# Layer normalisation and one rotary sum of the second layer's projection stage, moved to VectorE

## The chip, the cores and the metric

One core of a Trainium2 chip runs the whole program. The metric is the device time of one execution in microseconds (us), smaller is better. The engines are TensorE (PE, its weight loads PEld), VectorE (DVE), ScalarE (ACT), GpSimd (POOL) and SyncE (SP, which here only issues DMAs). They run apart from one another, each in its own program order, and meet at semaphores.

## The reference

Two layers over x, 4 sequences of 2048 tokens, 256 channels:

```
xn = layernorm(x); x = x + rwkv_attention(xn) * silu(relu_ffn(xn))            # layer 0
xn = layernorm(x)                                                              # layer 1
c_q = xn @ W_DQ;  q = [c_q @ W_UQ, rope(c_q @ W_QR)]
c_kv = xn @ W_DKV; k = [c_kv @ W_UK, rope(xn @ W_KR)];  v = c_kv @ W_UV
s = causal_softmax(q k^T / sqrt(24)) v @ W_O                                   # 16 heads
xr, xk = mu * xn + (1 - mu) * xn_previous_token                                # two mixes
g = silu(sigmoid(xr @ W_r) * (relu(xk @ W_k)^2 @ W_v));  x = x + s * g
```

with layernorm(x) = (x - mean) / sqrt(var + 1e-5). A product xhat = x * rstd + (-mean * rstd) and xhat = (x - mean) * rstd are two ways to write the same normalisation.

## The kernel before, in words

Four stages follow each other, parted by barriers: layer 0 (about 0 to 689 us), the projections of layer 1 (689 to 1062), attention, and the output. The change lies in the second, `layer1_projections`. It works through 16 chunks of 512 tokens (4 tiles of 128 tokens by 256 channels), numbered n = 0 to 15. Each engine's order is written out by hand in its own `body(b, c, left)`, and `left` is the number of chunks still to come (capped at 4), so the last chunks drop the steps that prepare later ones.

What one body of each engine does, for chunk n:

- DVE: low halves of the latents (L1343, it reads PSUM), rotary products of the keys (L1349), low half of the query content (L1352), rotary products of the queries into q_cos and q_sin (L1356), low half of the key content (L1359), low half of the rotary queries (L1362: q_cos minus its half-precision copy), then for chunk n+2 the statistics (L1260), for chunk n+1 the two mixes (L1276: x_k twice, x_r twice) with the aggregation of chunk n+2 (L1267) between them, the low half of x_k (L1283), and the gate's product (L1373).
- POOL: rotary sum of the keys (L1126), square (L1129), rotary sum of the queries q_cos += q_sin (L1131), for chunk n+1 the token difference (L1101) and the low half of xn (L1106), low half of the rotary keys (L1136), for chunk n+2 `rstd_of`: var + eps (L1090), shift = -mean (L1091), rstd by pow (L1093), shift * rstd (L1095); then the low half of x_r of chunk n+1 (L1110) and the gate of chunk n (L1145).
- ACT: evictions and half-precision copies; `normalise` of chunk n+2 (L1175: four ACTIVATEs of 128x256, scale rstd, bias shift) stands after the latents (L1217) and ahead of the gate's sigmoid (L1248), the relu (L1224) and the query eviction (L1227).
- PE: latents, rotary keys, x_k product (12 matmuls), query products (8), `transposes` of the next chunk's xhat (L1393), x_r products in two halves around the key content product (4 matmuls), values, and the last product.
- SP: per chunk 4 stores of query content (L1040), 2 of rotary keys (L1043), 4 of key content (L1048), 2 of rotary queries (L1051), 1 of values (L1053), 1 of the gate (L1056), in this order, each kind behind a wait on the producer; a load of x (L1062) ahead of them while chunks are left. After chunk 12 it also issues the 20 loads of attention's first operands (`load_group`, L1487 and L1491).

A "low half" is the rest that a half-precision copy leaves: f32 value minus f16 copy. Layer 0 has its own `normalise`, on DVE (L455: four TENSOR_SCALARs of 128x256, subtract the mean, multiply by rstd).

Of the kernel before, what the change touches and what calls it, by code (L numbers as in the profile page):

```python
# [850 lines left out]
def layer1_projections(nc, a, d, ident, rows_out, early, scales, first):  # L851
# [6 lines left out]
    with ExitStack() as ctx:  # L858
# [44 lines left out]
        shift = sb("b_shift", [P, TPC])  # L903
        zeros = sb("b_zeros", [P, TPC])
# [73 lines left out]
        qr_sum = sem("b_qr_sum")  # L978
# [43 lines left out]
        with nc.Block() as block:  # L1022
# [53 lines left out]
            def _(pool):  # L1076
# [6 lines left out]
                pool.memset(zeros[:], 0.0).then_inc(consts_set, 1)  # L1083
                pool.wait_ge(consts_set, 5)

                def rstd_of(n):
# [35 lines left out]
                def body(b, c, left):  # L1122
# [27 lines left out]
            def _(act):  # L1150
# [70 lines left out]
                def body(b, c, left):  # L1221
# [773 lines left out]
```

## Time and profile before

| what | value |
|---|---|
| runs | 2144.02, 2147.37, 2146.47 us (median 2146.47) |
| the profiled execution | 2144.02 us, of which the span is 2142.3 us |
| busy over the span | PE 92%, DVE 77%, ACT 75%, POOL 31% |
| the stage's steady stretch, 821 to 842 us | PE busy 17.94, DVE 16.97, ACT 13.69, POOL 17.67 of 21 us, granted TensorE clock 1.00 |

The page gives shares over the whole program; the stage's own shares come from the busy times by stretch. In a row of the timeline the first number is the start in us from the span's start, the second the length from the start of the first to the end of the last merged instruction ("x4" are four of them). A length includes time in which the instruction has begun but cannot go on. The clock was 1.00 of full speed, which is 2.4 GHz, in the steady stretch.

### The profile page before, as it was taken

The page shows a single profiled execution, that of the slowest core. Times are in us where ns is not written, and L with a number is a line of the kernel's source. Part 1 is how long each engine was busy: PE and PEld are TensorE (multiplying, and loading weights), DVE is VectorE, ACT ScalarE, POOL GpSimd, SP SyncE. Part 2 cuts the span into 40 slices and gives each one's busy share as a digit, 9 for nine tenths or more (in the row PEclk, how much of TensorE's full clock was granted, in tenths as well). Part 3 has the DMA queues.
Part 4 walks back from the last instruction along what each step waited for, and adds up shares of the span by engine and source line. Part 5 has one row for each costly group of instructions (what it writes and reads, how often), then busy time and mean ns, then how long its engine had stood idle before and what let it go on. Part 6 is the DMA issues. An engine that isn't in the chain of part 4 may idle for free. (4 is left out here: it accounts for less than half of the span.)

```text
span 2142.3 us, 54405 instructions
## 1 busy us (share of the span) xinstructions
PE 1973.6 (92%) x23334; PEld 997.8 (47%) x23334; DVE 1643.6 (77%) x2204; ACT 1605.4 (75%) x1897; POOL 667.2 (31%) x448
## 2 busy tenths in 40 slices
PE   5999999999997788888599999999999999999986
PEld 2655655665564445454334343334443333443335
DVE  7867667766745787878488888888888888888877
ACT  5545545544544666666499999999999999999972
POOL 1644653554555688888300000000000000000008
PEclk9999999999998899999899999999999999999999
DMA  3000100010021356566522222222212222221229
GB/s 102 20 20 20 37 24 20 24 37 20 21 70 51 107 159 197 152 196 167 172 66 71 59 67 67 67 71 70 72 57 66 69 67 59 59 61 39 71 82 320
DMA packets 134959, 170.24 MB, mean 79 GB/s; under 512 B 14528, under 2 KB 106432, under 8 KB 134464
## 3 DMA queue, kind: packets, MB, share of 16 engines
q1 hardware_dynamic: 132688, 164.53, 26.3%
q8 instruction: 185, 3.03, 0.6%
q10 hardware_dynamic: 2032, 2.24, 0.3%
q14 instruction: 54, 0.44, 0.1%
HBM read 91.21 MB, written 75.50 MB: 78 GB/s over the span
## 5 line engine op out<-in xcount | busy, mean ns | idle before, releaser
L1667 ACT ACTIVATE c_probs<-c_ps_b 128x1536 f32<-128x1536 f32 x544 | 858.5, 1578 | 0.0
L1779 PE MATMUL c_ps_o<-c_probs,c_v 128*32 128x256 f32 (+3 forms) x6656 | 581.9, 453 | 3.9 <-DVE c_probs L1699 0.8
L1699 DVE TENSOR_SCALAR c_probs<-c_probs 128x2048 f32<-128x2048 f32 (+2 forms) x415 | 433.8, 1055 | 70.1 <-ACT c_probs L1667 68.1
L1759 PE MATMUL c_ps_a<-c_qk 24*128 24x256 f16 (+2 forms) x2688 | 445.1, 292 | 34.3 <-PEq L1022 17.5
L1759 PE MATMUL c_ps_b<-c_qk 24*128 24x256 f16 (+2 forms) x8064 | 454.0, 294 | 0.0
L1666 ACT ACTIVATE c_probs<-c_ps_a 128x512 f32<-128x512 f32 x544 | 390.1, 717 | 3.8 <-PE c_ps_b L1759 2.3
L1759 PEld LDWEIGHTS c_ps_a<-c_qk 24*128 24x128 f16 x2688 | 206.3, 92 | 382.6 <-ACT c_probs L1667 187.5
L1926 POOL TENSOR_TENSOR d_prod<-d_prod,d_x 128x1024 f32<-128x1024 f32 x8 | 26.2, 3291 | 1025.3 <-DVE d_prod L1914 1025.3
L1779 PEld LDWEIGHTS c_ps_o<-c_probs,c_v 128*32 128x32 f32 x6656 | 161.7, 108 | 245.4 <-issue 126.3
L258 POOL TENSOR_TENSOR a_hidh<-a_hid,a_hidh 128x512 f16<-128x512 f32 x128 | 170.0, 1347 | 233.8 <-ACT a_hidh L356 229.9
L1704 DVE TENSOR_SCALAR c_probs<-c_probs 128x1536 f32<-128x1536 f32 (+2 forms) x208 | 164.5, 797 | 65.6 <-ACT c_probs L1667 63.6
L1759 PEld LDWEIGHTS c_ps_b<-c_qk 24*128 24x128 f16 x8064 | 212.4, 93 | 0.6 <-issue 0.2
L667 PE MATMUL a_ps<-a_xnh,a_w 128*128 128x512 f16 x768 | 172.0, 379 | 12.0 <-ACT a_hid L351 12.0
L667 PE MATMUL a_ps<-a_w,a_hidh 128*128 128x256 f16 x1536 | 170.4, 273 | 0.0
L1708 DVE SCALAR_TENSOR_TENSOR c_probs<-c_probs,c_caps 128x512 f32<-128x512 f32 x256 | 169.6, 683 | 0.0
L667 PEld LDWEIGHTS a_ps<-a_w,a_hidh 128*128 128x128 f16 x1536 | 150.2, 98 | 17.7 <-POOL a_hidh L258 0.2
L667 PEld LDWEIGHTS a_ps<-a_xnh,a_w 128*128 128x128 f16 x768 | 73.1, 97 | 105.0 <-ACT a_hid L351 19.9
L351 ACT ACTIVATE a_hid<-a_ps,a_b 128x512 f32<-128x512 f32 x128 | 86.1, 685 | 31.8 <-PE a_ps L667 25.7
L367 ACT ACTIVATE a_gp<-a_gp 128x1024 f32<-128x1024 f32 x16 | 16.9, 1058 | 122.3 <-DVE a_gp L531 122.3
L492 DVE TENSOR_TENSOR_SCAN a_mx<-a_decay,a_mx,a_ps 128x512 f32<-128x512 f32 x32 | 39.2, 1268 | 84.3 <-PE a_ps L667 84.2
L346 ACT ACTIVATE a_en<-a_en 128x1024 f32<-128x1024 f32 x16 | 17.0, 1060 | 114.5 <-DVE a_en L499 114.5
L531 DVE SCALAR_TENSOR_TENSOR a_gp<-a_ps,a_unscale,a_b 128x1024 f32<-128x1024 f32 x16 | 20.5, 1282 | 102.1 <-PE a_ps L667 102.0
(248 smaller groups left out, 2951.3 us busy)
## 6 DMA issues: line engine op xcount, KB each, us to landing
c_qk<-qk_d SPq DMA_DIRECT2D x256, 96.0 KB
v_d<-b_val SPq DMA_DIRECT2D x16, 1024.0 KB
c_v<-v_d SPq DMA_DIRECT2D x64, 256.0 KB
rows<-in_x SPq DMA_DIRECT2D x16, 512.0 KB, 4.8
x_d<-rows_out SPq DMA_DIRECT2D x16, 512.0 KB, 3.2
rows<-x_d SPq DMA_DIRECT2D x16, 512.0 KB, 6.3
qk_d<-b_qc SPq DMA_DIRECT2D x64, 128.0 KB
qk_d<-b_kc SPq DMA_DIRECT2D x64, 128.0 KB
```

The source lines that it names most:

```text
L258: nc.gpsimd.tensor_tensor(hid_half[:, 1, m], hid[:, m % RING], hid_half[:, 0, m], ALU.subtract).then_inc(hid_low, 1)
L351: nc.scalar.activation(hid[:, m % RING, :], ps_a[:, m % 2, :], ACT.Relu, bias=b_1[:, m:m + 1], scale=hid_scale).then_inc(hid_done, 1)
L492: nc.vector.tensor_tensor_scan(mx[:, k, 1:CH + 1], decay[:, k:k + 1].to_broadcast([P, CH]), ps_b[:, k, :], mx[:, k, 0:1], ALU.add, ALU.max ...
L667: mm = nc.tensor.matmul(ps, l, r, start=(first and i == 0), stop=(last and i == len(steps) - 1))
L1666: nc.scalar.activation(probs[:, t % NPROB, PARTS[0]], ps_a[:], ACT.Exp, scale=unscale).then_inc(exp_a_done, 1)
L1667: nc.scalar.activation(probs[:, t % NPROB, PARTS[1]], ps_b[:, t % 2], ACT.Exp, scale=unscale).then_inc(exp_b_done, 1)
L1699: nc.vector.tensor_scalar(tile, tile, P_MAX, P_MIN, ALU.min, ALU.max).then_inc(clip_done, 1)
L1704: nc.vector.tensor_scalar(tile[:, :, at:end], tile[:, :, at:end], P_MAX, P_MIN, ALU.min, ALU.max)
L1708: op = nc.vector.scalar_tensor_tensor(tile[:, :, at:at + P], tile[:, :, at:at + P], P_MIN, cap, ALU.max, ALU.min)
L1759: mm = nc.tensor.matmul(into, k[rows, hk, kt * P:(kt + 1) * P], tokens[rows, hq], start=(i == 0), stop=(i == len(TERMS) - 1), tile_positio ...
L1779: mm = nc.tensor.matmul(ps_o[j * VW:(j + 1) * VW, column:column + w], v[:, kt, j * VW:(j + 1) * VW], probs[:, step % NPROB, j, at:at + w], ...
L1926: nc.gpsimd.tensor_tensor(prod[:, n % OUT], prod[:, n % OUT], x1(n % SLOTS), ALU.add).then_inc(sum_done, 1)
```

## The change

`normalise` of layer 1 is taken from ACT and put on DVE, as four TENSOR_SCALARs of 128x256 that subtract the mean and multiply by rstd. For that, POOL's `rstd_of` loses the two shift instructions, the zeros and the wait for xhat. The sum q_cos += q_sin is taken from POOL and put on DVE, behind the two products that feed it; PE's wait for the products counts 3 per chunk instead of 2. In the prologue `normalise(0)` stands behind the weights' squares on DVE and `normalise(1)` behind the low half of chunk 0's x_k. SP's order is not changed.

```diff
-pool.wait_ge(consts_set, 5)
+pool.wait_ge(consts_set, 4)
 def rstd_of(n):
     pool.wait_ge(mv_done, TPC * n + TPC)
-    pool.wait_ge(xhat_done, TPC * n)
     nc.gpsimd.tensor_tensor(var_eps[:], mv[:, :, 1], eps[:], ALU.add).then_inc(rstd_done, 1)
-    nc.gpsimd.tensor_tensor(shift[:], zeros[:], mv[:, :, 0], ALU.subtract).then_inc(rstd_done, 1)
-    pool.wait_ge(rstd_done, 4 * n + 2)
+    pool.wait_ge(rstd_done, 2 * n + 1)
     nc.gpsimd.tensor_tensor(rstd[:], var_eps[:], half[:], ALU.pow).then_inc(rstd_done, 1)
-    pool.wait_ge(rstd_done, 4 * n + 3)
-    nc.gpsimd.tensor_tensor(shift[:], shift[:], rstd[:], ALU.mult).then_inc(rstd_done, 1)
 def diff_of(n, c, first=False):
     pool.wait_ge(xn_done, 2 * n + 2)
...
     nc.gpsimd.tensor_tensor(act_k[:], relu[:], relu[:], ALU.mult).then_inc(act_done, 1)
-    pool.wait_ge(qr_parts, 2 * n + 2)
-    nc.gpsimd.tensor_tensor(q_cos[:], q_cos[:], q_sin[:], ALU.add).then_inc(qr_sum, 1)
     if left >= 1:
         diff_of(n + 1, c + 1)
         xn_low_of(n + 1, c + 1)
...
 x_scale = load("b_x_scale", scale[:, X:X + 1])
-def normalise(n, c, first=False):
-    act.wait_ge(rstd_done, 4 * n + 4)
-    if not first:
-        act.wait_ge(xt_done, n)
-    for j in range(TPC):
-        nc.scalar.activation(xhat[:, j, :], x[:, c % XS, j, :], ACT.Identity, bias=shift[:, j:j + 1],
...
-    act.wait_ge(qr_sum, n + 1)
+    act.wait_ge(qr_parts, 3 * n + 3)
     nc.scalar.activation(qr[:, s, 0, :], q_cos[:], ACT.Copy).then_inc(qr_high, 1)
     act.wait_ge(r_mm, n + 1)
...
                          ps_val.rearrange("p j (g h e) -> p g j h e", g=GROUPS, h=GH), ACT.Copy, scale=v_factor).then_inc(val_done, 1)
     if left >= 1:
         mixed_high(n + 1)
         latents_high(n + 1)
...
         nc.vector.bn_stats(stats[:, j, :], x[:, c % XS, j, :]).then_inc(stats_done, 1)
-def aggregate(n):
-    if n:
-        dve.wait_ge(rstd_done, 4 * n - 2)
+def aggregate():
     for j in range(TPC):
         nc.vector.bn_aggr(mv[:, j, :], stats[:, j, :]).then_inc(mv_done, 1)
+def normalise(n, c, first=False):
+    dve.wait_ge(rstd_done, 2 * n + 2)
+    if not first:
+        dve.wait_ge(xt_done, n)
+    for j in range(TPC):
+        nc.vector.tensor_scalar(xhat[:, j, :], x[:, c % XS, j, :], mv[:, j, 0:1], rstd[:, j:j + 1],
+                                ALU.subtract, ALU.mult).then_inc(xhat_done, 1)
...
+aggregate()
 dve.wait_ge(weights_loaded, 16 * early.loads)
 for t, column, sq in normed:
     nc.vector.tensor_tensor_reduce(out=sq, in0=t, in1=t, scale=1.0, scalar=0.0, op0=ALU.mult, op1=ALU.add,
                                    accum_out=sums[:, column:column + 1]).then_inc(squares_done, 1)
+normalise(0, 0, first=True)
 dve.wait_ge(roots_done, 1)
...
     dve.wait_ge(w_high, j + 1)
     nc.vector.scalar_tensor_tensor(halves[:, 1], w, scale[:, i:i + 1], halves[:, 0], ALU.mult, ALU.subtract).then_inc(w_low, 1)
 mix(0, 0, first=True)
 xk_low_of(0)
+normalise(1, 1)
 dve.wait_ge(late_loaded, 48)
...
                                        ALU.mult, ALU.mult).then_inc(qr_parts, 1)
+    dve.wait_ge(qr_parts, 3 * n + 2)
+    nc.vector.tensor_tensor(q_cos[:], q_cos[:], q_sin[:], ALU.add).then_inc(qr_parts, 1)
     dve.wait_ge(kc_high, n + 1)
...
     if left >= 1:
-        mix(n + 1, c + 1, (lambda: aggregate(n + 2)) if left >= 2 else None)
+        mix(n + 1, c + 1, aggregate if left >= 2 else None)
         xk_low_of(n + 1)
+    if left >= 2:
+        normalise(n + 2, c + 2)
     dve.wait_ge(kv_mm, n + 1)
...
-    pe.wait_ge(qr_parts, 2 * n + 2)
+    pe.wait_ge(qr_parts, 3 * n + 2)
     for j in range(TPC):
```

DVE, the steady loop, before: from the last rotary product of a chunk to the latents of the next (b_xhat is what `normalise` writes, b_gi the gate's product, b_lat the latents).

```order
L1356 SCALAR_TENSOR_TENSOR b_qsin<-b_ps,b_factor,b_sin 128x512
L1359 SCALAR_TENSOR_TENSOR b_kc<-b_ps,b_factor,b_kc 128x1024
L1362 TENSOR_TENSOR b_qr<-b_qcos,b_qr 128x512
L1260 BN_STATS b_stats<-rows 128x6 x4
L1276 SCALAR_TENSOR_TENSOR b_xk<-b_diff,b_mixes,b_xn 128x512 x2
L1267 BN_AGGR b_mv<-b_stats 128x2 x4
L1276 SCALAR_TENSOR_TENSOR b_xr<-b_diff,b_mixes,b_xn 128x512 x2
L1283 TENSOR_TENSOR b_xkh<-b_xk,b_xkh 128x1024
L1373 TENSOR_TENSOR b_gi<-b_ps,b_sigr 128x1024
L1343 SCALAR_TENSOR_TENSOR b_lat<-b_ps,b_factor,b_lat 64x512 x2
```

The same place in the changed kernel.

```order
L1343 SCALAR_TENSOR_TENSOR b_qsin<-b_ps,b_factor,b_sin 128x512
L1346 TENSOR_TENSOR b_qcos<-b_qcos,b_qsin 128x512
L1348 SCALAR_TENSOR_TENSOR b_kc<-b_ps,b_factor,b_kc 128x1024
L1351 TENSOR_TENSOR b_qr<-b_qcos,b_qr 128x512
L1237 BN_STATS b_stats<-rows 128x6 x4
L1259 SCALAR_TENSOR_TENSOR b_xk<-b_diff,b_mixes,b_xn 128x512 x2
L1242 BN_AGGR b_mv<-b_stats 128x2 x4
L1259 SCALAR_TENSOR_TENSOR b_xr<-b_diff,b_mixes,b_xn 128x512 x2
L1266 TENSOR_TENSOR b_xkh<-b_xk,b_xkh 128x1024
L1249 TENSOR_SCALAR b_xhat<-rows,b_mv,b_rstd 128x256 x4
L1364 TENSOR_TENSOR b_gi<-b_ps,b_sigr 128x1024
L1330 SCALAR_TENSOR_TENSOR b_lat<-b_ps,b_factor,b_lat 64x512 x2
```

Five instructions per chunk are new on DVE: one ahead of the key content's low half, four between the low half of x_k and the gate's product.

POOL, the steady loop, before: from the square to the gate.

```order
L1129 TENSOR_TENSOR b_actk<-b_relu 128x1024
L1131 TENSOR_TENSOR b_qcos<-b_qcos,b_qsin 128x512
L1101 TENSOR_TENSOR b_diff<-b_xn 128x1024
L1106 TENSOR_TENSOR b_xnh<-b_xn,b_xnh 128x1024
L1136 TENSOR_TENSOR b_kr<-b_kcos,b_kr 8x512
L1090 TENSOR_TENSOR b_var<-b_mv,b_eps 128x4
L1091 TENSOR_TENSOR b_shift<-b_zeros,b_mv 128x4
L1093 TENSOR_TENSOR b_rstd<-b_var,b_half 128x4
L1095 TENSOR_TENSOR b_shift<-b_shift,b_rstd 128x4
L1110 TENSOR_TENSOR b_xrh<-b_xr,b_xrh 128x1024
L1145 TENSOR_TENSOR rows_out<-b_gi,b_gs 128x1024
```

The same place in the changed kernel.

```order
L1121 TENSOR_TENSOR b_actk<-b_relu 128x1024
L1093 TENSOR_TENSOR b_diff<-b_xn 128x1024
L1098 TENSOR_TENSOR b_xnh<-b_xn,b_xnh 128x1024
L1126 TENSOR_TENSOR b_kr<-b_kcos,b_kr 8x512
L1085 TENSOR_TENSOR b_var<-b_mv,b_eps 128x4
L1087 TENSOR_TENSOR b_rstd<-b_var,b_half 128x4
L1102 TENSOR_TENSOR b_xrh<-b_xr,b_xrh 128x1024
L1135 TENSOR_TENSOR rows_out<-b_gi,b_gs 128x1024
```

Three instructions per chunk are gone from POOL, and the low half of x_r (b_xrh) now follows the pow directly.

## Rows read from the trace of the kernel before

**Rows 1.** The timeline of DVE over one chunk (start, length, engine, line, operation, out<-in).
```profile
797.41 0.37 DVE L1267 BATCH_NORM_AGGREGATE b_mv<-b_stats 128x2 f32<-128x6 f32 x4
799.00 1.22 DVE L1283 TENSOR_TENSOR b_xkh<-b_xk,b_xkh 128x1024 f16<-128x1024 f32 x1
...
801.38 1.43 DVE L1343 SCALAR_TENSOR_TENSOR b_lat<-b_ps,b_factor,b_lat 64x512 f16<-64x512 f32 x2
...
806.56 1.28 DVE L1352 SCALAR_TENSOR_TENSOR b_qc<-b_ps,b_factor,b_qc 128x1024 f16<-128x1024 f32 x1 [2.21 <-ACT b_qc L1227]
...
810.03 1.28 DVE L1359 SCALAR_TENSOR_TENSOR b_kc<-b_ps,b_factor,b_kc 128x1024 f16<-128x1024 f32 x1 [0.87 <-ACT b_kc L1231]
812.13 3.73 DVE L1362 TENSOR_TENSOR b_qr<-b_qcos,b_qr 128x512 f16<-128x512 f32 x1 [0.81 <-ACT b_qr L1235]
...
818.54 0.37 DVE L1267 BATCH_NORM_AGGREGATE b_mv<-b_stats 128x2 f32<-128x6 f32 x4
```

**Rows 2.** The timeline of POOL over the same chunk.
```profile
798.43 1.84 POOL L1091 TENSOR_TENSOR b_shift<-b_zeros,b_mv 128x4 f32<-128x4 f32 x1
...
801.61 2.13 POOL L1110 TENSOR_TENSOR b_xrh<-b_xr,b_xrh 128x1024 f16<-128x1024 f32 x1
804.79 2.36 POOL L1145 TENSOR_TENSOR rows_out<-b_gi,b_gs 128x1024 f32<-128x1024 f32 x1 [1.05 <-ACT b_gs L1248]
...
808.33 1.88 POOL L1129 TENSOR_TENSOR b_actk<-b_relu 128x1024 f32<-128x1024 f32 x1
810.18 1.25 POOL L1131 TENSOR_TENSOR b_qcos<-b_qcos,b_qsin 128x512 f32<-128x512 f32 x1
811.40 1.89 POOL L1101 TENSOR_TENSOR b_diff<-b_xn 128x1024 f32<-128x1024 f32 x1
813.25 2.05 POOL L1106 TENSOR_TENSOR b_xnh<-b_xn,b_xnh 128x1024 f16<-128x1024 f32 x1
815.27 1.59 POOL L1136 TENSOR_TENSOR b_kr<-b_kcos,b_kr 8x512 f16<-8x512 f32 x1
```

**Rows 3.** The timeline of ACT and PE in the same chunk.
```profile
801.69 2.08 ACT L1175 ACTIVATE b_xhat<-rows,b_shift,b_rstd 128x256 f32<-128x256 f32 x4 [0.55 <-POOL b_shift L1095]
...
803.67 1.04 ACT L1248 ACTIVATE b_gs<-b_gi 128x1024 f32<-128x1024 f32 x1
...
807.90 1.04 PE L1400 MATMUL b_ps<-b_lat,b_wuk 128*128 128x512 f16 x4 [0.74 <-DVE b_qc L1352]
...
808.98 1.02 ACT L1231 ACTIVATE b_kc<-b_ps 128x1024 f16<-128x1024 f32 x1 [0.54 <-PE b_ps L1400]
```

**Rows 4.** Two lines on DVE: instructions, minimum/median/maximum in ns, first and last start.
```profile
L455 DVE TENSOR_SCALAR a_xhat<-rows,a_mv,a_rstd x64: 401/1244/2504, 15.5 to 586.1; 128x256 f32<-128x256 f32 x64
L1362 DVE TENSOR_TENSOR b_qr<-b_qcos,b_qr x16: 1005/3728/3740, 728.7 to 1041.6; 128x512 f16<-128x512 f32 x16
```

**Rows 5.** The timeline of layer 0 where its normalise runs, DVE and POOL.
```profile
419.76 4.03 DVE L455 TENSOR_SCALAR a_xhat<-rows,a_mv,a_rstd 128x256 f32<-128x256 f32 x4
418.57 6.24 POOL L258 TENSOR_TENSOR a_hidh<-a_hid,a_hidh 128x512 f16<-128x512 f32 x5 [1.44 <-ACT a_hidh L356]
```

**Rows 6.** The timeline of chunk 0, DVE and POOL.
```profile
727.61 1.89 POOL L1101 TENSOR_TENSOR b_diff<-b_xn 128x1024 f32<-128x1024 f32 x1
728.75 1.30 DVE L1362 TENSOR_TENSOR b_qr<-b_qcos,b_qr 128x512 f16<-128x512 f32 x1
```

**Rows 7.** The timeline of the stage's prologue, four engines apart.
```profile
693.60 3.51 POOL L1113 MEMSET b_val<- 128x4096 f32 x1
...
694.08 3.06 DVE L1295 TENSOR_SCALAR b_bound<-b_roots 128x9 f32<-128x9 f32 x1 [0.97 <-ACT b_roots L1158]
...
703.50 0.21 ACT L1188 ACTIVATE b_xn<-b_zero 128x2 f32<-128x2 f32 x1 [2.12 <-PE b_ps L1393]
...
710.13 0.74 DVE L1332 SCALAR_TENSOR_TENSOR b_wk<-b_gs,b_scale,b_wk 128x512 f16<-128x512 f32 x1
...
710.35 1.39 POOL L1093 TENSOR_TENSOR b_rstd<-b_var,b_half 128x4 f32<-128x4 f32 x1
```

**Rows 8.** The timeline of SP's queue: chunk 12's and chunk 15's gate stores.
```profile
997.44 0.39 SPq L1056 DMA_DIRECT2D gate_d<-rows_out  x1
...
1057.97 0.54 SPq L1056 DMA_DIRECT2D gate_d<-rows_out  x1
```

**Rows 9.** Whom SP's queue waited for in the stage (us, times, longest).
```profile
SPq L1056 <- POOL rows_out L1145: 23.1, 13, 2.2
```

More of the change, by code:

```diff
@@ L902, in layer1_projections @@
         rstd = sb("b_rstd", [P, TPC])
-        shift = sb("b_shift", [P, TPC])
-        zeros = sb("b_zeros", [P, TPC])
         xhat = sb("b_xhat", [P, TPC, DIM])
@@ L977, in layer1_projections @@
         qr_parts = sem("b_qr_parts")
-        qr_sum = sem("b_qr_sum")
         qr_high = sem("b_qr_high")
@@ L1082, in _ @@
                 pool.memset(eps[:], LN_EPS).then_inc(consts_set, 1)
-                pool.memset(zeros[:], 0.0).then_inc(consts_set, 1)
-                pool.wait_ge(consts_set, 5)
+                pool.wait_ge(consts_set, 4)
                 def rstd_of(n):
                     pool.wait_ge(mv_done, TPC * n + TPC)
-                    pool.wait_ge(xhat_done, TPC * n)
                     nc.gpsimd.tensor_tensor(var_eps[:], mv[:, :, 1], eps[:], ALU.add).then_inc(rstd_done, 1)
-                    nc.gpsimd.tensor_tensor(shift[:], zeros[:], mv[:, :, 0], ALU.subtract).then_inc(rstd_done, 1)
-                    pool.wait_ge(rstd_done, 4 * n + 2)
+                    pool.wait_ge(rstd_done, 2 * n + 1)
                     nc.gpsimd.tensor_tensor(rstd[:], var_eps[:], half[:], ALU.pow).then_inc(rstd_done, 1)
-                    pool.wait_ge(rstd_done, 4 * n + 3)
-                    nc.gpsimd.tensor_tensor(shift[:], shift[:], rstd[:], ALU.mult).then_inc(rstd_done, 1)
                 def diff_of(n, c, first=False):
@@ L1113, in _ @@
                 pool.memset(val[:], 0.0).then_inc(consts_set, 1)
-                pool.wait_ge(consts_set, 6)
+                pool.wait_ge(consts_set, 5)
                 for s in range(2):
@@ L1167, in _ @@
                 x_scale = load("b_x_scale", scale[:, X:X + 1])
-                def normalise(n, c, first=False):
-                    act.wait_ge(rstd_done, 4 * n + 4)
-                    if not first:
-                        act.wait_ge(xt_done, n)
-                    for j in range(TPC):
-                        nc.scalar.activation(xhat[:, j, :], x[:, c % XS, j, :], ACT.Identity, bias=shift[:, j:j + 1],
-                                             scale=rstd[:, j:j + 1]).then_inc(xhat_done, 1)
                 def xn_of(n, c):
@@ L1200, in mixed_high @@
                     nc.scalar.activation(xr_half[:, 0], x_r[:], ACT.Copy).then_inc(xr_high, 1)
-                normalise(0, 0, first=True)
                 xn_of(0, 0)
@@ L1210, in _ @@
                 mixed_high(0, first=True)
-                normalise(1, 1)
                 def latents_high(n):
@@ L1238, in body @@
                     act.wait_ge(val_mm, n + 1)
-                    act.wait_ge(consts_set, 8)
+                    act.wait_ge(consts_set, 7)
                     nc.scalar.activation(val[:, s, :, :, :, 0:D_H].rearrange("p g j h e -> p g (j h) e"),
@@ L1244, in body @@
                         latents_high(n + 1)
-                    if left >= 2:
-                        normalise(n + 2, c + 2)
                     act.wait_ge(gate_in_done, n + 1 + 1)
@@ L1286, in _ @@
                 dve.wait_ge(stats_done, TPC)
-                aggregate(0)
+                aggregate()
                 dve.wait_ge(weights_loaded, 16 * early.loads)
@@ L1328, in _ @@
                 dve.wait_ge(scale_done, 1)
-                aggregate(1)
+                aggregate()
                 for j, (w, halves, i) in enumerate(parts):
```

## The prediction

> **What bounds the kernel now.** I read the busy shares by stage, then the timeline of one chunk in the projection stage on each engine, then the two lines that matter most, and last SP's waits. No engine is full there (PE 17.94, DVE 16.97, POOL 17.67 of 21 us in the table above), so a chain of waits sets the pace. Two marks close it into a loop: M, where the aggregation ends (797.41 + 0.37 = 797.78), and L, where the latents' low halves end (801.38 + 1.43 = 802.81) [rows 1]. From M to L it takes 5.03 us, from L to the end of the rotary low half (812.13 + 3.73 = 815.86) 13.05, from there to the next M (818.54 + 0.37 = 818.91) 3.05: together 21.13 us per chunk.
>
> Two of its pieces are waits for POOL inside a DVE instruction. The rotary low half takes 3.73 us in the steady loop and 1.005 at least; the median of 16 is 3.728 [rows 1, 4]. It begins during the token difference of POOL (811.40 to 813.29), sits through that and the low half of xn (813.25 to 815.30), and ends 0.56 us later [rows 2]. In chunk 0 it sits through one only: the difference ends at 729.50, the DVE instruction at 730.05, 0.55 later [rows 6]. So a two-input DVE instruction waits through one POOL instruction, sometimes through two, and then needs 0.55 us. It goes the other way too: POOL's four-column shift starts at M + 0.65 and takes 1.84 us; it ends at 800.27, 0.05 after x_k's low half leaves DVE at 800.22 [rows 1, 2].
>
> The stage's end hangs on something else. SP waited for the gate 13 times, so in chunks 0 to 12 [rows 9]; from chunk 12's gate store at 997.44 to the last store's issue at 1058.51 it is 61.07 us, in which SP issues without a pause (20 loads and three chunks of stores) [rows 8]. What moves the end is when the gate of chunk 12 is ready; what the three chunks after it gain is lost behind SP.
>
> **The change, part by part.**
>
> *ScalarE loses four ACTIVATEs* (2.08 us) that stand ahead of sigmoid, relu and query eviction [rows 3]. Before, the query content's low half begins at 806.56, L + 3.75, held by ACT. After, ACT waits for PE: four matmuls until ACT starts are 1.08 us (807.90 to 808.98), the eviction 1.02 [rows 3], with 0.1 of handing over L + 2.2. It ends at L + 3.5, the two rotary products at L + 4.8.
>
> *VectorE gains the rotary sum*, a two-input instruction of 128x512. POOL at that time: the gate starts after the product's end (L - 1.46) plus sigmoid 1.04, at L - 0.3, and ends 2.36 later at L + 2.05; the square starts 1.18 after (from 807.15 to 808.33 before), at L + 3.2, and ends at L + 5.1 [rows 2]. So the sum begins at L + 4.8 and ends at 5.1 + 0.55 = L + 5.65. The key content's low half begins after that in any case: before it was at 810.03, L + 7.22, and PE had idled 0.74 us for DVE ahead of its product [rows 1, 3]; with that gone it begins at L + 6.55 and ends at L + 7.85. The sum therefore costs nothing on the chain; if it sits through two POOL instructions it ends at L + 7.5 and the key content comes 0.9 later, still under cover of what follows. Less than nothing is bounded by the 0.81 us that DVE idled ahead of the rotary low half [rows 1].
>
> *POOL loses that sum* (1.25 us [rows 2]): the difference runs from L + 5.05, gives 0.5 to DVE's sum, ends at L + 7.5; the low half of xn ends at L + 9.55. The rotary low half on DVE, ready at L + 7.8, waits for that and ends at L + 10.1. Against 13.05 this saves 2.95.
>
> *The normalisation on VectorE* is what pays this back. It can't start before the pow. The pow stands where the shift stood, and I take it that its read is held as the shift's was, to M + 2.44 (800.22). What a pow needs after release is 0.87: at 710.35 + 1.39 = 711.74 one ended, 0.87 after the DVE instruction that held it (710.13 + 0.74) [rows 7]. So rstd is ready at M + 3.31. POOL's low half of x_r, already free to go, follows within a few hundredths, as it now follows the second shift at 801.61, and holds 2.13 us, to M + 5.4 [rows 2]. The four TENSOR_SCALARs are the same form as layer 0's, whose 64 take 401 to 2504 ns, median 1244, though 401 is the length undisturbed [rows 4]; beside a busy POOL four take 4.03 us [rows 5]. Here POOL has nothing more to run until the gate, which waits for DVE, so one POOL instruction is waited for, and then 1.1 us is spent (at most 4 x 0.40 = 1.6; the first has already begun and starts overlap). End M + 6.5. The gate's product takes 1.16 (800.22 to 801.38), the latents 1.43 [rows 1]: L lies at M + 9.1, 4.07 later than before. The whole normalisation is thus bounded by 1.1 and 4.03 us on DVE; I take 3.2 after rstd. Queued behind it are the gate's product and the latents, and for these PE waits (its query products) and ACT (sigmoid).
>
> Period: 9.1 + 10.1 + 3.05 = 22.25, against 21.13: 1.12 us slower. Chunks 0 to 12 make 13 such periods: +14.6 us.
>
> *Gate against SP.* Chunk 12's gate ends at L + 2.05 instead of L + 4.34 (807.15): -2.3 us.
>
> *Prologue.* ACT's first copy of xn waits for PE's transposes until 703.50 [rows 7], since ACT's normalisation came after the scales. In the change DVE does it during its wait for the square roots, behind POOL's memset: the memset holds such instructions, as 3.06 us for 9 columns show [rows 7]. That pushes the scales by about 0.8 (1.1 less 0.3 of spare), but takes 2.08 and the 2.12 us of waiting for the transposes off ACT: 3.4 earlier. `normalise(1)`, behind chunk 0's x_k and split by a 2.13 us POOL instruction, gives 0.5 back (bounds 0 and 3). Net -2.9 us, between 0 and -4.
>
> Sum: +14.6 - 2.3 - 2.9 = +9.4 us. The profiled execution took 2144.0 us: 2153.4. The median shown lies 2.5 us above that execution, and some of it may come along; I say 2154.
>
> Of the lock the Trainium skill has a rule (SBUF — State Buffer, Who interferes with whom): an instruction that gets the pair of ports shared by the two engines keeps it for its whole length, and who issues first decides. The trace agrees with the first half only: the rotary low half was issued at 812.13, before xn's low half at 813.25, and lost all the same [rows 1, 2]; by the rule it would have ended at 813.84.
>
> **The rivals.**
>
> 1. *The pow reads in the gap at M + 1.30*, between two DVE instructions, and ends at M + 2.17. Then the low half of x_r starts at M + 2.5, when ACT's copy is ready, almost together with the first TENSOR_SCALAR; one of the two still waits, but the four end at M + 5.55 and L is M + 8.15. Period 21.3, 13 x 0.17 = 2.2, sum -3.0: 2141. For it: the pow is issued ahead of x_k's low half. Against: the shift was too, and lost. By the skill's rule (same section) the first to issue wins, which makes this rival the forecast.
>
> 2. *DVE gets the port before the low half of x_r.* rstd at M + 3.31, four instructions to 4.7, L at M + 7.3, period 20.45: 13 x -0.68 - 5.2 = -14: 2130. It decides at the moment when rstd is ready: DVE must issue before POOL's next. Against it: POOL's next starts at 801.61, before the shift ahead of it ends at 801.65, and ACT's waiting instruction only at 801.69 [rows 2, 3].
>
> 3. *The rotary low half again sits through two POOL instructions*, xn's and the rotary keys' (1.15 us without the part in which it waits itself [rows 2], 1.59 less 0.45). Then 1.1 more per period, +14.6: 2168. For it: that is what it does now in the steady loop; against: chunk 0.
>
> **How the numbers follow.** Forecast 0.46, rival 1 0.26, rival 2 0.11, rival 3 0.17. The range 2137 to 2169 leaves out rival 2 and the edges of the others, nearly 2 in 10; the forecast's own is 2149 to 2159. What can be told from no change is 0.2% (4.3 us). Faster by more: rival 2 and a third of rival 1, 0.20. Within: the rest of rival 1 and the forecast's low edge, 0.23. Slower: 0.57.
>
> **What the profile after would show.** A period of 22.2 us between aggregations; the TENSOR_SCALARs of the normalisation in about 3.2 us for four, the first over 2 us; the pow near 2.5 us long (rival 1: 1.4); the rotary low half near 2.3 us instead of 3.73; xn's first copy near 700 us; SP without a wait behind chunk 12's gate. If SP waits again in the last chunks, the end is no longer SP's; if the four TENSOR_SCALARs take under 1.5 us, rival 2 is right and the sum is wrong by its largest term.

## The result

The changed kernel takes 2174.76 us (median; 2173.04 to 2175.99) against 2146.47 (2144.02 to 2147.37): a ratio of 1.0133, 95% interval [1.0115, 1.0150]. The forecast was 2154 with a range of 2137 to 2169. Its sign is right and its size is not: 28 us slower instead of 7.5. The profiled execution took 2176.74 us with a span of 2175.0 (before 2144.0 and 2142.3).

The marks are those of the prediction: M, the end of the aggregation, and L, the end of the latents' low halves. First VectorE over one chunk of the changed kernel, the timeline that answers to [rows 1] (start, length, engine, line, operation, out<-in); L is at 812.25 + 0.75 = 813.00.

```profile
812.25 0.75 DVE L1330 SCALAR_TENSOR_TENSOR b_lat<-b_ps,b_factor,b_lat 64x512 f16<-64x512 f32 x1
...
815.36 1.28 DVE L1339 SCALAR_TENSOR_TENSOR b_qc<-b_ps,b_factor,b_qc 128x1024 f16<-128x1024 f32 x1 [0.81 <-ACT b_qc L1206]
...
818.00 4.56 DVE L1346 TENSOR_TENSOR b_qcos<-b_qcos,b_qsin 128x512 f32<-128x512 f32 x1
822.48 1.27 DVE L1348 SCALAR_TENSOR_TENSOR b_kc<-b_ps,b_factor,b_kc 128x1024 f16<-128x1024 f32 x1
823.68 0.67 DVE L1351 TENSOR_TENSOR b_qr<-b_qcos,b_qr 128x512 f16<-128x512 f32 x1
...
827.03 0.37 DVE L1242 BATCH_NORM_AGGREGATE b_mv<-b_stats 128x2 f32<-128x6 f32 x4
...
830.75 3.18 DVE L1249 TENSOR_SCALAR b_xhat<-rows,b_mv,b_rstd 128x256 f32<-128x256 f32 x4 [0.91 <-POOL b_rstd L1087]
...
835.09 1.43 DVE L1330 SCALAR_TENSOR_TENSOR b_lat<-b_ps,b_factor,b_lat 64x512 f16<-64x512 f32 x2
```

GpSimd in the same chunk answers to [rows 2]:

```profile
816.25 1.89 POOL L1121 TENSOR_TENSOR b_actk<-b_relu 128x1024 f32<-128x1024 f32 x1
818.10 1.88 POOL L1093 TENSOR_TENSOR b_diff<-b_xn 128x1024 f32<-128x1024 f32 x1
819.96 2.05 POOL L1098 TENSOR_TENSOR b_xnh<-b_xn,b_xnh 128x1024 f16<-128x1024 f32 x1
821.97 1.59 POOL L1126 TENSOR_TENSOR b_kr<-b_kcos,b_kr 8x512 f16<-8x512 f32 x1
...
828.18 2.53 POOL L1087 TENSOR_TENSOR b_rstd<-b_var,b_half 128x4 f32<-128x4 f32 x1
830.69 2.12 POOL L1102 TENSOR_TENSOR b_xrh<-b_xr,b_xrh 128x1024 f16<-128x1024 f32 x1
```

The rotary low half has shrunk from 3.73 us to 0.67. The sum, which now stands two instructions ahead of it, takes 4.56. It begins 0.14 us before the square ends (818.14), and sits through the difference and the low half of xn as well, to 822.01; it ends 0.55 later, the same 0.55 as in the kernel before. It is like this in the whole stage. The line of the sum (count, then minimum/median/maximum in ns):

```profile
L1346 DVE TENSOR_TENSOR b_qcos<-b_qcos,b_qsin x16: 692/4586/4601, 724.6 to 1077.1; 128x512 f32<-128x512 f32 x16
```

The 692 is chunk 15, where GpSimd has no further difference to run. Behind the sum stand VectorE's low half of the key content, and behind it TensorE; and ScalarE waits for the sum itself (both timelines, idle time in brackets):

```profile
822.59 0.63 ACT L1214 ACTIVATE b_qr<-b_qcos 128x512 f16<-128x512 f32 x1 [2.91 <-DVE b_qcos L1346]
```

```profile
823.81 6.55 PE L1454 MATMUL b_ps<-b_wv,b_actk 128*128 128x256 f32 x16 [3.51 <-DVE b_kc L1348]
```

TensorE's product takes 6.55 us here instead of 3.72. The granted clock was 0.50 there, the level of 1.2 GHz, after TensorE had idled 3.51 us (columns: window, busy us with counts for PE, weight loads, DVE, ACT, POOL, then the clock, the DMA share and GB/s).

```profile
824.00:827.00 3.00, 3.00 (x8) 2.37 (x9) 2.96 (x7) 1.05 (x2) 0.00 (x0) 0.50 0.36 43
```

This costs nothing in the changed kernel: in chunks 2, 11 and 12 the same product ran in 3.72 us, and their periods are 23.52 to 23.54 like all others. They also show that the idle time alone doesn't tell what the clock will be. Chunk 2 had idled as long and ran at 1.00:

```profile
776.76 3.72 PE L1454 MATMUL b_ps<-b_wv,b_actk 128*128 128x256 f32 x16 [3.54 <-DVE b_kc L1348]
```

In the experiments below this clock does cost time, where it meets another product.

Last, SP's waits and its stores, which answer to [rows 9] and [rows 8]. The gate is now waited for 14 times. Chunk 12's store is issued 29.4 us later than before (997.44), and the last one of the stage at 1088.94, 31.0 later. Behind chunk 14's gate, for which it waited 1.9 us, SP waited twice more, 3.0 us for chunk 15's query content (the store at 1075.77) and 1.4 for its rotary keys (1079.65).

```profile
SPq L1053 <- POOL rows_out L1135: 71.7, 14, 5.6
```

```profile
1026.82 0.39 SPq L1053 DMA_DIRECT2D gate_d<-rows_out  x1
...
1072.36 0.39 SPq L1053 DMA_DIRECT2D gate_d<-rows_out  x1
1075.77 2.47 SPq L1037 DMA_DIRECT2D qk_d<-b_qc  x4
1079.65 0.73 SPq L1040 DMA_DIRECT2D qk_d<-b_kr  x2
...
1088.94 0.68 SPq L1053 DMA_DIRECT2D gate_d<-rows_out  x1
```

### The profile page after: what moved, and what is told of

It is laid out like the page before. It is cut to its first block and busy times, and to the rows that moved or that the text cites. A ratio compares the mean times of both kernels' runs of the same rounds, so it can differ in the third digit from the quotient of the medians.

```text
span 2175.0 us, 54357 instructions
## 1 busy us (share of the span) xinstructions
PE 1996.0 (92%) x23334; PEld 1020.2 (47%) x23334; DVE 1712.5 (79%) x2284; ACT 1579.7 (73%) x1833; POOL 639.4 (29%) x399
## 5 line engine op out<-in xcount | busy, mean ns | idle before, releaser
L1454 PE MATMUL b_ps<-b_wv,b_actk 128*128 128x256 f32 x256 | 85.3, 506 | 52.2 <-DVE b_kc L1348 52.2
L367 ACT ACTIVATE a_gp<-a_gp 128x1024 f32<-128x1024 f32 x16 | 16.9, 1058 | 122.3 <-DVE a_gp L531 122.3
```

The lines of the kernel that those rows point to most:

```text
L1454: mm = nc.tensor.matmul(ps_kv[:, j, :], act_k[:, k, j * P:(j + 1) * P], w_v[:, k, :], start=(k == 0), stop=(k == KT - 1))
```

## The experiments

All ratios are against the kernel before on the same chip, with 95% intervals. M to L and L to M are read from each kernel's timeline in the steady loop.

| kernel | median us | ratio | M to L | L to M | period |
|---|---|---|---|---|---|
| before | 2146.47 | | 5.03 | 16.11 | 21.14 |
| changed | 2174.76 | 1.0133 [1.0115, 1.0150] | 9.12 | 14.40 | 23.52 |
| sum back on GpSimd | 2170.15 | 1.0107 [1.0090, 1.0124] | 9.12 | 13.1 to 14.6 | 22.2 to 23.7 |
| normalisation back on ScalarE | 2183.31 | 1.0169 [1.0152, 1.0186] | 7.0 | 16.9 | 23.90 |
| changed, sum's operand in PSUM | 2158.41 | 1.0051 [1.0034, 1.0068] | 9.12 | 13.0 to 13.3 (one 14.25) | 22.1 to 22.4 (one 23.4) |
| changed, normalisation ahead of x_r | 2147.33 | 1.0006 [0.9996, 1.0015] | 7.32 | 13.07 (4 of 13), 14.3 to 14.4 | 20.39, 21.6 to 21.7 |
| both of these | 2132.42 | 0.9939 [0.9925, 0.9952] | 7.32 | 12.6 (10 of 13), 13.4 | 19.92, 20.7 |
| before, sum on VectorE with PSUM | 2129.86 | 0.9927 [0.9914, 0.9941] | 5.03 | 14.87 | 19.90 |
| the same, sum's result in PSUM too | 2116.41 | 0.9857 [0.9842, 0.9872] | 5.03 | 13.67 | 18.70 |
| before, small instruction ahead of the rotary low half | 2145.15 | 0.9998 [0.9989, 1.0007] | 5.03 | 16.10 | 21.13 |
| before, keys' low half ahead of xn's | 2138.99 | 0.9966 [0.9952, 0.9980] | 5.03 | 15.59 | 20.62 |
| changed, keys' sum behind the difference | 2179.70 | 1.0153 [1.0139, 1.0167] | 9.12 | 14.8 to 15.1 | 23.9 to 24.2 |

**The two halves of the change apart.** The sum goes back to GpSimd, the rest stays:

```diff
+ pool.wait_ge(qr_parts, 3 * n + 2)
+ nc.gpsimd.tensor_tensor(q_cos[:], q_cos[:], q_sin[:], ALU.add).then_inc(qr_parts, 1)
...
- dve.wait_ge(qr_parts, 3 * n + 2)
- nc.vector.tensor_tensor(q_cos[:], q_cos[:], q_sin[:], ALU.add).then_inc(qr_parts, 1)
```

> Only the normalisation is on VectorE; the rotary sum goes back to GpSimd. Theory A (a two-input VectorE instruction sits through the whole run of GpSimd instructions that follow each other without a pause, up to the 8-partition one, and the sum's 4.56 us is what the prediction missed): the rotary low half again waits through xn's low half (about L + 10.75 at its end), period 9.1 + 10.75 + 3.05 = 22.9 us, time about 2163 us. Rival B (the normalisation alone makes the slow-down, the sum is harmless): period 23.5, time as the changed kernel, 2175 us. Rival C (the sum is nearly all of it): period near 21.5, time about 2148 us.

Measured 2170.15, between theory A and rival B, and far from rival C. M to L is 9.12 as in the changed kernel. From L to M the chunks differ, from 13.09 us in chunk 8 to 14.61 in chunks 1 and 12, and TensorE's clock goes with it. In each of chunks 1 to 13 TensorE idles 3.1 to 4.0 us for the latents and then runs the query products; chunks 3 and 8 (the second and third lines are of one window each, columns as above):

```profile
788.80 3.57 PE L1391 MATMUL b_ps<-b_lat,b_wq 128*128 128x512 f16 x8 [3.16 <-DVE b_lat L1332]
789.00:792.00 3.00, 3.00 (x8) 1.11 (x7) 1.34 (x3) 1.23 (x2) 3.00 (x3) 0.50 0.77 290
905.50:907.20 1.70, 1.70 (x9) 0.79 (x9) 1.29 (x2) 0.97 (x2) 1.70 (x1) 1.00 1.04 398
905.42 1.89 PE L1391 MATMUL b_ps<-b_lat,b_wq 128*128 128x512 f16 x8 [3.50 <-DVE b_lat L1332]
```

At a granted clock of 0.50 they take 3.57 us, and L to M takes 14.60; at 1.00 they take 1.89 and L to M 13.09. ScalarE's evictions, the rotary products and GpSimd's sum stand behind them. At full clock a smaller wait is left: the rotary low half ends early, and the mixes of x_k wait instead, 2.68 us for 1.4 in chunk 8 and in chunk 4, which is shown here:

```profile
821.04 0.87 DVE L1351 TENSOR_TENSOR b_qr<-b_qcos,b_qr 128x512 f16<-128x512 f32 x1
...
823.26 2.68 DVE L1261 SCALAR_TENSOR_TENSOR b_xk<-b_diff,b_mixes,b_xn 128x512 f32<-128x512 f32 x2
```

And the normalisation returns to ScalarE, with the shift on GpSimd, while the sum stays on VectorE (`normalise` and `rstd_of` as in the kernel before):

> Only the sum is on VectorE; the normalisation stays on ScalarE. Theory A: the sum starts at L + 6.4 and sits through square, difference and xn's low half, to about L + 11.8, so 5.4 us long; the rotary low half then takes 0.68; the end is at L + 13.7 against 13.05 before, period 21.7 us, time about 2152 us. Rival B: the sum is harmless, period 21.1, 2146 us. Rival C: period above 23, 2172 us.

Measured 2183.31, slower than the whole change. The sum's end, L + 12.0, is what theory A said (11.8); the time is beyond rival C's 2172, for a reason that none of the three had. The sum takes 4.70 us again, and it is asked for later (L + 7.3), since ScalarE is late with the query's eviction. TensorE then idles 3.66 us and runs its product at a granted clock of 0.50 (824.00 to 828.20 had 0.90, 828.30 to 834.20 has 0.50), and here that counts: the gate's product waits for TensorE (0.60 us), the latents for ScalarE behind TensorE (0.70 and 0.54), and M to L grows from 5.03 to 7.0. The product is 2.9 us longer than at full clock. It ran at the lower clock in chunks 0 to 14 of this kernel, so no period at full clock stands beside it. VectorE and TensorE, two timelines:

```profile
822.33 4.70 DVE L1356 TENSOR_TENSOR b_qcos<-b_qcos,b_qsin 128x512 f32<-128x512 f32 x1
```

```profile
828.28 6.60 PE L1462 MATMUL b_ps<-b_wv,b_actk 128*128 128x256 f32 x16 [3.66 <-DVE b_kc L1358]
```

So each half alone costs 24 to 37 us, and the costs don't add. A part of that is the lower clock: it falls on the query products in the first kernel, on the last product in the second, and in the whole change on a product with slack.

**The sum without its wait.** The cosine product stays in PSUM, and the sum reads one operand from there:

```diff
- for i, (t_q, table) in enumerate(((q_cos, cos), (q_sin, sin))):
+ for i, (t_q, table) in enumerate(((ps_a[:, 0, :], cos), (q_sin[:], sin))):
...
- nc.vector.tensor_tensor(q_cos[:], q_cos[:], q_sin[:], ALU.add).then_inc(qr_parts, 1)
+ nc.vector.tensor_tensor(q_cos[:], ps_a[:, 0, :], q_sin[:], ALU.add).then_inc(qr_parts, 1)
...
- pe.wait_ge(qr_parts, 3 * n + 2)
+ pe.wait_ge(qr_parts, 3 * n + 3)
```

> The changed kernel, but the cosine product is written in place in PSUM and the sum reads one PSUM and one SBUF input; TensorE waits for the sum instead of the two products. Theory A: the sum takes 0.7 us, the wait goes back to the rotary low half, which ends 0.55 after xn's low half at about L + 9.5; period 9.1 + 9.5 + 3.05 = 21.7 us, time about 2149 us. Rival (the wait is not from the second SBUF input but from the semaphore or from GpSimd's writes): the sum stays at 4.5 us, period 23.5, 2175 us.

Measured 2158.41, 16 us of the 28 back: theory A's wait, and 9 us more than its time. VectorE's timeline of one chunk (L is 807.36):

```profile
812.33 0.69 DVE L1346 TENSOR_TENSOR b_qcos<-b_ps,b_qsin 128x512 f32<-128x512 f32 x1
815.21 1.28 DVE L1348 SCALAR_TENSOR_TENSOR b_kc<-b_ps,b_factor,b_kc 128x1024 f16<-128x1024 f32 x1 [2.19 <-ACT b_kc L1210]
816.41 1.02 DVE L1351 TENSOR_TENSOR b_qr<-b_qcos,b_qr 128x512 f16<-128x512 f32 x1
```

The sum takes 0.69 us in all 16 chunks, so its wait came with the second operand in SBUF. The rotary low half ends at 817.43, L + 10.07, where the prediction had L + 10.1; that they agree is chance (at full clock, in the kernel with both waits away, it ends at L + 9.56). The key content's low half waits 2.19 us here, and behind that stands TensorE's clock again: after 3.07 us of idle the query products take 2.45 us instead of 1.89 (granted clock 0.50 from 808.80 to 811.20), and in chunks 1 to 14 they take 2.35 to 3.57.

```profile
807.51 2.45 PE L1391 MATMUL b_ps<-b_lat,b_wq 128*128 128x512 f16 x8 [3.07 <-DVE b_lat L1330]
```

**The normalisation without its wait.** GpSimd's low half of x_r waits until the rows are normalised:

```diff
 def xr_low_of(n):
     pool.wait_ge(xr_high, n + 1)
+    if n and n + 1 < NCH:
+        pool.wait_ge(xhat_done, TPC * (n + 1) + TPC)
```

> The changed kernel, but GpSimd's low half of x_r also waits until the normalisation of that round is done, so that VectorE gets the ports first. Theory A: the four TENSOR_SCALARs take 1.4 us instead of 3.18, L lies at M + 7.3 instead of 9.1, period 21.7 us, time about 2152 us. Rival B (the lock at this place costs nothing since something else ends as late): period stays at 23.5, time 2175 us.

Measured 2147.33, no different from the kernel before; theory A had 2152. The four instructions take 1.38 us instead of 3.18 (VectorE, then GpSimd), though each of them reads only one large operand from SBUF:

```profile
821.43 1.38 DVE L1251 TENSOR_SCALAR b_xhat<-rows,b_mv,b_rstd 128x256 f32<-128x256 f32 x4 [0.91 <-POOL b_rstd L1087]
...
831.25 1.69 DVE L1348 TENSOR_TENSOR b_qcos<-b_qcos,b_qsin 128x512 f32<-128x512 f32 x1
```

```profile
822.96 2.14 POOL L1104 TENSOR_TENSOR b_xrh<-b_xr,b_xrh 128x1024 f16<-128x1024 f32 x1 [1.56 <-DVE b_xhat L1251]
...
830.50 1.88 POOL L1093 TENSOR_TENSOR b_diff<-b_xn 128x1024 f32<-128x1024 f32 x1
```

In every second chunk the sum was asked for a little later in GpSimd's row, during the difference, and took 1.69 us instead of 4.58. The line at 831.25 is such a sum, and it raised the question of the next experiment.

**Does the moment decide how many instructions are waited for?** A small instruction in the kernel before moves the rotary low half's start from 0.73 to 0.82 us into the difference:

```diff
...
  dve.wait_ge(qr_high, n + 1)
+ nc.vector.bn_aggr(spare[:], ones[:, 0:6])
  nc.vector.tensor_tensor(qr[:, s, 1, :], q_cos[:], qr[:, s, 0, :], ALU.subtract).then_inc(qr_low, 1)
```

> The kernel before, with nothing moved: one small operation of VectorE (two columns, the aggregation of a row of ones into a spare tile) stands ahead of the rotation's low half, so that this instruction is asked for a little later, about 0.80 us or more after GpSimd began the difference instead of 0.73. Theory (whether a two-input instruction of VectorE gets in at the end of GpSimd's running instruction, or waits through the next one too, hangs on when in the running one it is asked for): the low half gets in behind the difference and takes about 1.8 us instead of 3.73, as in chunk 0 (1.30). The mixes' wait for GpSimd's later work then takes part of the gain, as in chunk 0, where the next aggregation ended 4.3 us behind it: the period goes from 21.1 to about 20.4, the time to about 2136 us. Rival (the order of the instructions sets it, not the moment): the low half still takes 3.7 us, the period stays 21.1 to 21.2 and the time 2147 to 2149.

Measured 2145.15, ratio 0.9998 [0.9989, 1.0007]. The theory of the moment, as it was put, fell: the low half lost in 14 chunks as before, and the rival's 3.7 us and unchanged period were measured.

```profile
812.25 0.18 DVE L1364 BATCH_NORM_AGGREGATE b_spare<-b_ones 128x2 f32<-128x6 f32 x1 [0.82 <-ACT b_qr L1236]
812.35 3.63 DVE L1365 TENSOR_TENSOR b_qr<-b_qcos,b_qr 128x512 f16<-128x512 f32 x1
```

**Is it what stands next on GpSimd?** In the kernel before, the keys' low half and the low half of xn are exchanged, so an 8-partition instruction follows the difference:

```diff
  if left >= 1:
      diff_of(n + 1, c + 1)
-     xn_low_of(n + 1, c + 1)
  pool.wait_ge(kr_high, n + 1)
  nc.gpsimd.tensor_tensor(kr[:, s, 1, :], k_cos[:], kr[:, s, 0, :], ALU.subtract).then_inc(kr_low, 1)
+ if left >= 1:
+     xn_low_of(n + 1, c + 1)
```

> The kernel before with two of GpSimd's instructions exchanged: the rotary keys' low half (8 partitions) now stands between the difference and the inputs' low half. In the traces so far a two-input instruction of VectorE asked for during the difference mostly waited through the inputs' low half too, whatever the moment it was asked, but one asked for during the inputs' low half always got in ahead of the rotary keys' 8-partition instruction behind it. Theory (what stands next on GpSimd decides; an 8-partition instruction lets VectorE in): the rotation's low half takes about 1.7 us instead of 3.73. The mixes then meet the inputs' low half, which is later by 1.2 us or more, and wait for it: period 20.3 to 21.0, time 2136 to 2145 us. Rival (the low half waits through two of GpSimd's instructions whatever they are): it takes 2.9 us, period 21.5 or more since the inputs' low half is late for TensorE, time 2150 us or more.

Measured 2138.99, ratio 0.9966 [0.9952, 0.9980]. The time and the period (20.62) are the theory's, the wait is the rival's: the low half sat through the difference and the 8-partition instruction, 2.83 us, and gained 0.9 only because that one is short (VectorE, then GpSimd).

```profile
811.38 2.83 DVE L1363 TENSOR_TENSOR b_qr<-b_qcos,b_qr 128x512 f16<-128x512 f32 x1 [0.83 <-ACT b_qr L1236]
```

```profile
810.65 1.88 POOL L1101 TENSOR_TENSOR b_diff<-b_xn 128x1024 f32<-128x1024 f32 x1
812.50 1.15 POOL L1135 TENSOR_TENSOR b_kr<-b_kcos,b_kr 8x512 f16<-8x512 f32 x1
```

The like was done to the changed kernel, with the sum of the rotary keys moved between the difference and the low half of xn (`k_cos` stands behind `diff_of`):

> The changed kernel with GpSimd's sum of the rotary keys (8 partitions) moved from the head of its chunk to between the difference and the inputs' low half, so that the square and the difference start 1.3 us sooner and an 8-partition instruction stands where the sum on VectorE is waiting. Theory (as for the exchange in the kernel before): the sum gets in behind the difference, takes about 1.7 us instead of 4.58 and ends about 6.7 us behind the latents' low halves; the cosine keys' low halves end at 7.9, the rotation's low half waits 0.5 to 1.5 us for the inputs' low half, the next aggregation comes about 13.0 us behind instead of 14.40; period 22.1, time about 2157 us. Rival (the sum waits through two instructions whatever they are): it ends at 7.9 or later, ScalarE is late for the rotary rows, period 23.0 or more, time 2168 us or more.

Measured 2179.70, ratio 1.0153 [1.0139, 1.0167]: the theory's wait, and the rival's period and time. The sum did get in behind the difference this time, 2.25 us instead of 4.58. The expectation was wrong about the rest. The difference doesn't start sooner, since it waits for ScalarE's copy of xn; that waits for TensorE's transposes, and they stand behind query products that take 3.31 us instead of 1.89, after 3.98 us of idle and at a granted clock of 0.54 (814.00 to 817.00). And ScalarE's high half of the keys waits for the moved sum. The rotary low half begins at L + 10.4 (GpSimd, ScalarE and VectorE):

```profile
819.33 1.89 POOL L1093 TENSOR_TENSOR b_diff<-b_xn 128x1024 f32<-128x1024 f32 x1 [1.71 <-ACT b_xn L1170]
```

```profile
822.92 0.63 ACT L1212 ACTIVATE b_kr<-b_kcos 8x512 f16<-8x512 f32 x1 [1.65 <-POOL b_kcos L1122]
```

```profile
819.52 2.25 DVE L1346 TENSOR_TENSOR b_qcos<-b_qcos,b_qsin 128x512 f32<-128x512 f32 x1
...
824.10 1.36 DVE L1351 TENSOR_TENSOR b_qr<-b_qcos,b_qr 128x512 f16<-128x512 f32 x1 [1.13 <-ACT b_qr L1214]
```

**Both waits away**, in the changed kernel: the sum's operand in PSUM, and GpSimd's low half of x_r behind the normalisation:

> The changed kernel with both suspected costs taken away: the cosine product is put in PSUM, so the sum on VectorE reads one operand from SBUF only, and GpSimd's low half of the rotary inputs waits until the normalisation is written. Theory (the changed kernel's period is longer by the sum's wait and by the four normalisations' wait, each separately): the end of the aggregation to the end of the latents' low halves 7.3 us as with the second edit alone, from there to the next aggregation 13.1 as with the first alone, period 20.4, time about 2133 us. Rival (something else bounds it near the kernel before's period, TensorE or the keys): period 21.1 or more, time 2146 or more.

Measured 2132.42, the theory's 2133. The gains add up: the two alone gave 16 and 27 us, together 42. In ten chunks the query products run at full clock, 1.89 us; there the rotary low half ends at L + 9.56 and L to M is 12.61. In the three others they take 2.6 to 3.2 us at a clock that is in part 0.50, and L to M is 13.3 to 13.4: the price of the clock within one kernel. A chunk at full clock (L is 797.89):

```profile
805.26 2.18 DVE L1353 TENSOR_TENSOR b_qr<-b_qcos,b_qr 128x512 f16<-128x512 f32 x1
...
810.13 0.37 DVE L1244 BATCH_NORM_AGGREGATE b_mv<-b_stats 128x2 f32<-128x6 f32 x4
```

**The sum's move alone, without its wait**, in the kernel before (normalisation on ScalarE):

> The kernel before with the normalisation left on ScalarE, and the sum on VectorE with its first operand in PSUM. It tells whether the sum's place on VectorE costs anything once it needs no SBUF operand pair. Theory (the cost was the wait of the sum, not its place): the sum takes 0.7 us, the cosine keys end 7.2 us behind the latents' low halves, the rotation's low half is asked for about 1.05 us into the difference and gets in behind it; period 18 to 20, where TensorE becomes the bound; time 2125 to 2132 us. Rival (the wait moves to the rotation's low half, and that waits through two of GpSimd's instructions again): the low half ends 11.8 us behind the latents' low halves, period 19.9 to 21.2, time 2128 to 2147.

Measured 2129.86. M to L is 5.03 as before, and 16 us are gained. The rotary low half starts 1.05 us into the difference and loses all the same, 3.41 us, so it ends at L + 11.8 and the period is 19.90: the rival's numbers. So its operand was put in PSUM as well, in a bank that is free there:

```diff
- nc.scalar.activation(qr[:, s, 0, :], q_cos[:], ACT.Copy).then_inc(qr_high, 1)
+ nc.scalar.activation(qr[:, s, 0, :], ps_t[:, 1, :], ACT.Copy).then_inc(qr_high, 1)
...
+ dve.wait_ge(xn_high, n + 2 if left >= 1 else n + 1)
- nc.vector.tensor_tensor(q_cos[:], ps_a[:, 0, :], q_sin[:], ALU.add).then_inc(qr_parts, 1)
+ nc.vector.tensor_tensor(ps_t[:, 1, :], ps_a[:, 0, :], q_sin[:], ALU.add).then_inc(qr_parts, 1)
...
- nc.vector.tensor_tensor(qr[:, s, 1, :], q_cos[:], qr[:, s, 0, :], ALU.subtract).then_inc(qr_low, 1)
+ nc.vector.tensor_tensor(qr[:, s, 1, :], ps_t[:, 1, :], qr[:, s, 0, :], ALU.subtract).then_inc(qr_low, 1)
```

> The kernel before with the normalisation on ScalarE, and the sum on VectorE with both its cosine operand and its result in PSUM, so that the rotation's low half reads one operand from PSUM and one from SBUF. Theory (an instruction of VectorE with one operand in PSUM doesn't wait for GpSimd): the rotation's low half takes 0.7 us instead of 3.41, and the statistics start 2.7 us sooner; the first mix then waits for the inputs' low half of GpSimd (asked for during it, so it gets in ahead of the rotary keys) and the second for the rotary keys' low half, as in chunk 0 of the kernel before; the next aggregation comes about 13.5 us behind the latents' low halves instead of 14.87, period 18.5, time about 2112 us. Rival (TensorE or GpSimd bounds it): TensorE is busy 17.75 of 19.90 us of the period with the normalisation on ScalarE and one sum in PSUM, and follows the keys' rows; if its gaps stay, the period is 19.5 or more and the time 2125 us or more.

Measured 2116.41 (the theory had 2112), the fastest of all: 30 us below the kernel before. The low half takes 0.68 us; the mixes, the next with two operands in SBUF, take 2.94 instead of 1.42.

```profile
800.77 0.70 DVE L1356 TENSOR_TENSOR b_ps<-b_ps,b_qsin 128x512 f32<-128x512 f32 x1
...
802.81 0.68 DVE L1361 TENSOR_TENSOR b_qr<-b_ps,b_qr 128x512 f16<-128x512 f32 x1
...
804.84 2.94 DVE L1272 SCALAR_TENSOR_TENSOR b_xk<-b_diff,b_mixes,b_xn 128x512 f32<-128x512 f32 x2
```

## Why the prediction was wrong

**The step that failed** is "The sum therefore costs nothing on the chain", with its end at L + 5.65, one GpSimd instruction behind its start. Its start was right (L + 5.00 for 4.8). It ended at L + 9.56, because it lost not only to the square but to the difference and the low half of xn. The text allowed for two instructions and for L + 7.5, "still under cover"; a wait for three was not considered, although one for two stood in [rows 1, 2] as the steady state. The low half of the key content came at L + 9.48 instead of 6.55, and from L to M it took 14.40 instead of 13.15: 1.25 us per chunk. With this wait taken away the kernel ran in 2158.41 us, with its query products partly at the lower clock. With the normalisation's wait gone too, L to M was 12.61 in the chunks at full clock. The rival that came nearest, a second long wait in the rotary low half at 2168, had nearly the right cost (1.1 us per period) in the wrong instruction: the rotary low half took 0.67 us, where near 2.3 was forecast.

**What hid a part of it.** The forecast let the difference lose 0.5 us to the sum and so had xn's low half end at L + 9.55. The difference lost nothing (1.88 us long), and xn's low half ended at L + 9.01. By this alone the forecast was 0.54 us per chunk too long. Against the 12.61 of the kernel with both waits away, the sum's wait costs 1.8 us per chunk, and not 1.25. (The L + 6.55 for the key content is 6.48 by its own terms, 7.22 less 0.74; nothing hangs on it.)

**The same step, by periods.** 13 equal periods were counted, but chunk 0 was no such period before: its rotary low half took 1.30 us [rows 6], its period 18.02. It grew by 5.1 us to 23.13, the twelve others by 2.38 each, 28.6: together 33.7. From this go 2.1 us by which chunk 0 reaches L earlier (719.31 for 721.37) and 2.3 for the gate; the rest, 29.3, is to 0.1 us the 29.4 by which chunk 12's gate store is late. SP's own tail of 61.07 us [rows 8] became 62.8 (to 1089.62). It no longer issues without a pause: it waited for chunk 14's gate and for chunk 15's query content and keys, 6.3 us in all. That is the sign the prediction named for the end being no longer SP's, and it came; it was worth the 1.7 us. Chunk 0 was worth 4 us of the error (5.1 instead of 1.12).

**What held.** M to L: 9.12 for 9.1. The pow took 2.53 us for near 2.5, so it was held as the shift had been, and rival 1 is out. GpSimd's low half of x_r began 0.06 us ahead of VectorE's first instruction of the normalisation, so rival 2 is out as well; the four took 3.18 us for 3.2. The query content's low half began at L + 2.36 for 2.2. The gate of chunk 12 counted 2.3. In the prologue the stage began 0.9 us later on the clock of the trace and reached its first L 2.1 earlier, 2.9 for 2.9. From the end of the rotary low half to M it took 3.05, as before. The price of 4.07 for M to L is confirmed from the other side: with the order on GpSimd changed, M to L fell by 1.8.

**The rule of the Trainium skill** (SBUF — State Buffer, Who interferes with whom) that who issues first gets the ports is contradicted here a second time, and more plainly: the sum began at 818.00, before the difference and before xn's low half, and ended behind both. The same section says that a VectorE instruction with at most one input in SBUF, outside the modes that use two ports, doesn't contend with GpSimd, and with that the runs of the sum and of the low half agree: 0.69 us in place of 4.58, 0.68 in place of 3.41.

**What stays open** is which of GpSimd's row an instruction of VectorE gets in behind. Asked for during the difference with xn's low half next, it waited for that too when it came up to 0.73 us after the difference's start (0.02, 0.07, 0.24, 0.26, 0.54, 0.73), and at 0.82; it didn't at 0.75, 0.85, 1.14, 1.23 and 1.57; at 1.05 both are seen. So early askers lost and late ones got in, but between 0.75 and 1.05 the moment doesn't decide. Nor does the kind of the next instruction (8 partitions: lost in 14 chunks, won in 13 of another kernel). Three patterns had no exception in these runs: asked for in the last 0.3 us of the square, the sum lost to the difference and to xn's low half as well (32 times in three kernels); asked for during the low half of xn, or during that of the rotary keys, an instruction got in behind that one. What decides the clock that TensorE gets after an idle time is open too: nearly the same idle time was followed by both levels within one kernel.

## What to carry to other kernels

When VectorE and GpSimd both run instructions with two operands in SBUF, price each of VectorE's by the whole unbroken row that GpSimd has in front of it, not by the one instruction that is running; a wait for two in the profile is a warning that three can come. Taking such an instruction off one engine doesn't remove the wait, it hands it to the next one in the row, and with it to whatever that one feeds. Putting one operand in PSUM does remove it: with the sum alone moved to VectorE the kernel lost 37 us; with one operand of it in PSUM it gained 16, and with its result there too, 30. One large operand in SBUF is no safeguard for every instruction, as the normalisation's four show (3.18 us for 1.38). When a wait is taken away, look where TensorE idles afterwards and which product comes behind it. And before multiplying by the number of chunks, look at the first period by itself.

## What the runs showed of the hardware

- A 128x512 sum of two SBUF operands on VectorE took 0.69 us alone and up to 4.70 beside GpSimd; it always ended 0.55 us behind the instruction that it had lost to last.
- Four 128x256 TENSOR_SCALARs, with one large operand in SBUF, took 1.38 us when GpSimd's low half of x_r was held back and 3.18 beside it.
- After TensorE had idled 3.51 us its next product ran at a granted clock of 0.50 and took 6.55 us instead of 3.72; in three other chunks it idled 3.54 or 3.55 us and ran at 1.00. The lower clock cost nothing where TensorE had slack. In front of the query products it made L to M 14.60 us instead of 13.09 (the sum on GpSimd, chunks 3 and 8) and 13.4 instead of 12.6 (both waits away), there after only 2.15 us of idle.
